# Residual tiles held in the turned rows' order, row norms of later batches on ScalarE, and two x buffers instead of three

## What is computed

```python
x = x + attention(layernorm(x))        # Q, K, V, scores / sqrt(256) * gaussian mask over keys, softmax, V, Wo, bo
x = x + ffn(layernorm(x))              # h = gelu(x @ bw1.T + b1), out = h @ bw2.T + b2, hidden width 1024
# bw = mean(|w|, axis=1) * sign(w), for w1 and w2
```

## Time and profile before

| | |
|---|---|
| median of 3 executions | 1831.75 us |
| lowest, highest | 1826.61, 1834.94 us |
| the profiled execution | 1829.88 us |
| its span | 1828.1 us |
| mean granted TensorE clock | 0.935 of full speed |
| busy: TensorE, VectorE, ScalarE, GpSimd | 1534.9, 1128.3, 885.6, 1243.6 us |
| share of the span | 84%, 62%, 48%, 68% |
| DMA | 121.70 MB, 30.2% of 16 engines |

### The profile page before, as it was taken

One profiled execution on the slowest core, in us unless ns is written; L12 is line 12 of the kernel. 1 busy time (PEld: TensorE's weight loads), 2 busy tenths in 40 slices (PEclk: granted clock), 3 DMA queues, 4 the chain that ended last, 5 costly groups with the idle time before them and its releaser, 6 DMA issues. The chain is left out here.

```text
span 1828.1 us, 20907 instructions
## 1 busy us (share of the span) xinstructions
PE 1534.9 (84%) x7645; PEld 1290.1 (71%) x7645; DVE 1128.3 (62%) x1560; ACT 885.6 (48%) x1118; POOL 1243.6 (68%) x1281
## 2 busy tenths in 40 slices
PE   7787878888788887998788887888798888888887
PEld 5677767777667766777677776776677766776777
DVE  6665666656667565765556656566665666755635
ACT  4554544545455354553535545454554545535443
POOL 4958677576776767767587765867757577675634
PEclk8889998999999899999989988999999999989999
DMA  4504324042340424305143141332404234051220
GB/s 144 111 16 72 91 46 107 9 85 78 56 105 8 85 70 70 93 14 91 58 70 93 32 80 51 70 92 41 105 17 81 81 52 110 1 92 46 47 70 23
DMA packets 103330, 121.70 MB, mean 67 GB/s; under 512 B 11310, under 2 KB 94652, under 8 KB 103228
## 3 DMA queue, kind: packets, MB, share of 16 engines
q1 hardware_dynamic: 103200, 120.37, 30.2%
q10 hardware_dynamic: 28, 0.01, 0.0%
HBM read 20.72 MB, written 16.78 MB: 21 GB/s over the span
## 5 line engine op out<-in xcount | busy, mean ns | idle before, releaser
L379 POOL TENSOR_TENSOR probs<-probs 128x512 fp32r<-128x512 f32 x256 | 351.2, 1390 | 162.9 <-ACT probs L504 162.2
L995 PE MATMUL ps<-sgn,probs 128*128 128x256 f32 x1024 | 284.8, 311 | 99.0 <-DVE ys L729 99.0
L685 DVE STREAM_TRANSPOSE probs<-probs 128x1024 f32<-128x1024 f32 x128 | 159.1, 1243 | 268.5 <-DMA probs<-g 268.1
L504 ACT ACTIVATE probs<-probs 128x1024 fp32r<-128x1024 f32 x128 | 135.6, 1060 | 361.4 <-DVE probs L685 361.4
L995 PEld LDWEIGHTS ps<-sgn,probs 128*128 128x128 f32 x1024 | 222.7, 217 | 110.5 <-issue 72.6
L929 PE MATMUL ps<-probs,xnh 128*128 128x512 f32 x1024 | 283.6, 391 | 0.0
L996 PE MATMUL ps<-sgn,probs 128*128 128x256 f32 x1024 | 279.7, 306 | 0.0
L498 ACT ACTIVATE g<-ps,nmax 128x1024 f32<-128x1024 f32 x128 | 142.6, 1115 | 171.6 <-DVE nmax L677 129.2
L996 PEld LDWEIGHTS ps<-sgn,probs 128*128 128x128 f32 x1024 | 222.4, 217 | 0.8
L929 PEld LDWEIGHTS ps<-probs,xnh 128*128 128x128 f32 x1024 | 190.0, 188 | 38.0
L982 PE MATMUL ps<-rows_h,sgn 128*128 128x512 f32 x512 | 208.0, 406 | 8.6 <-DVE xin L702 6.9
(11 more groups left out here) (112 smaller groups left out, 2967.4 us busy)
## 6 DMA issues: line engine op xcount, KB each, us to landing
probs<-g SPq DMA_DIRECT2D x512, 128.0 KB, 3.5
xin<-in_L_attn_x_dram SPq DMA_DIRECT2D x32, 512.0 KB, 4.6
out_dram<-xin SPq DMA_DIRECT2D x31, 512.0 KB, 3.9
regrouped_rows<-xn SPq DMA_DIRECT2D x120, 128.0 KB, 3.4
w1s<-in_L_ffn_w_dram SPq DMA_DIRECT2D x1, 1024.0 KB, 8.2
w2s<-in_L_ffn_w_dram SPq DMA_DIRECT2D x1, 1024.0 KB, 10.6
mask_bc<-mask_dram SPq DMA_DIRECT2D x1, 512.0 KB, 9.2
out_dram<-xin SPq DMA_DIRECT2D x1, 384.0 KB, 2.5
```

The source lines that it names most:

```text
L379: pool.tensor_tensor(ptl(q)[:, half(n)], pt(q)[:, half(n)], pth(q)[:, half(n)].bitcast(F32), ALU.subtract).then_inc(ptl_set, 1)
L685: dve.transpose(pt(q).rearrange("p (j g c) -> p g j c", j=T, c=QUAD), regrouped(q).rearrange("p (g j r) -> p g j r", j=T, r=QUAD)).then_in ...
L995: pe.matmul(bank, probs[:, 0, r, tile(j)], sgn2[:, j, :], start=j == 0, stop=False)
```

## The change

Six things are changed.

1. **The turned order is kept** for rows, queries and outputs: `hi_rows`, `lo_rows`, `hi_outputs` and `lo_outputs` copy without strides. `hi_keys` and `split_keys` still put the keys in natural order. The residual tiles `xin` are loaded in the order in which outputs now come (`x_res`: partition 8e + u holds the eight rows from 128u + 8e), and stored from it (`out_v`). For the first layernorm a second copy of x in the old order is loaded into one new buffer `xrow`. `xin` has two slots instead of three.
2. **SP's list**: `load_rows(b + 2)` (old order, into `xrow`) and `load(b + 1)` (into `xin`) stand where `load(b + 2)` stood; `regroup_rows(b + 2, n)` moves behind `regroup_probs(b + 1, 1)` and `(b + 1, 2)`.
3. **GpSimd** loses `normalize_attention`; ScalarE does it, four tiles behind each of the first two exponentials of b + 1, with a bias that VectorE makes (`center_attention`). `add_bias` keeps its place and now waits for `x_loaded`. `split_keys(b + 1, 0)` moves behind two `rstd_ffn`, `split_keys(b + 1, 1)` behind `lo_probs(b, 7)`, which moves behind four `rstd_ffn`.
4. **Row sums** of the exponentials are brought into the new order by one small matmul with a permutation matrix `perm` in each `project`; `invert_sums` reads its result.
5. **Query copies** move ahead: ScalarE copies query groups 0 and 1 around `hi_probs(b, 6)`, before `hi_outputs(b, 0)`, and VectorE takes their low parts before `lo_outputs(b, 0)`; `hi_keys` comes after `hi_probs(b, 7)`.
6. **Hidden pairs**: `hidden_pair(b, 3)` moves ahead of `turn_rows_ffn(b, 1)`; the exponentials use the `g` slots shifted by two, and wait for 6, 7 and 8 split pairs instead of 8 each. The preparation of weights before batch 0 is put in another order, the turning of sgn2 moves into batch 0, and mean |w1| is taken later.

```diff
-X_SLOTS = 3
+X_SLOTS = 2
+UNITS = 8
     x_v = x.rearrange("b (p t) d -> b p t d", t=T)
-    out_v = out.rearrange("b (p t) d -> b p t d", t=T)
+    x_res = x.rearrange("b (u e t) d -> b e u t d", u=UNITS, t=T)
+    out_v = out.rearrange("b (u e t) d -> b e u t d", u=UNITS, t=T)
...
-            return g[:, q % G_SLOTS, :]
+            return g[:, (q + 2) % G_SLOTS, :]
...
+            def load_rows(b, n):
+                if b > 0:
+                    sp.wait_ge(xn1_set, T * b)
+                sp.dma_start(xrow[:, n * TH:(n + 1) * TH, :],
+                             x_v[b, :, n * TH:(n + 1) * TH, :]).then_inc(row_loaded[n], 16)
...
                 if b == X_SLOTS - 1:
                     sp.wait_ge(sgn2_set, J // 2)
-                else:
+                elif b >= X_SLOTS:
                     sp.wait_ge(y_stored[n], 16 * (b - X_SLOTS + 1))
                 sp.dma_start(xin[s][:, n * TH:(n + 1) * TH, :],
-                             x_v[b, :, n * TH:(n + 1) * TH, :]).then_inc(x_loaded[s][n], 16)
+                             x_res[b, :, :, n * TH:(n + 1) * TH, :]).then_inc(x_loaded[s][n], 16)
...
                 if b + 2 < B:
                     for n in range(N2):
-                        load(b + 2, n)
+                        load_rows(b + 2, n)
+                if b + 1 < B:
                     for n in range(N2):
-                        regroup_rows(b + 2, n)
-                if b + 1 < B:
+                        load(b + 1, n)
                     for q in range(TH):
                         regroup_probs(b + 1, q)
+                        if q > 0 and q <= N2 and b + 2 < B:
+                            regroup_rows(b + 2, q - 1)
...
             def add_bias(b, tiles):
                 s = b % X_SLOTS
-                pool.wait_ge(xn1_set, T * (b + 1))
                 for t in tiles:
+                    if t % TH == 0:
+                        pool.wait_ge(x_loaded[s][t // TH], 16 * (b // X_SLOTS + 1))
...
                 lo_probs(b, 5)
                 lo_probs(b, 6)
-                if more:
-                    split_keys(b + 1)
                 rstd_ffn(b, 0)
-                lo_probs(b, 7, (0,))
                 rstd_ffn(b, 1)
-                lo_probs(b, 7, (1,))
+                if more:
+                    split_keys(b + 1, 0)
                 rstd_ffn(b, 2)
                 rstd_ffn(b, 3)
+                lo_probs(b, 7)
+                if more:
+                    split_keys(b + 1, 1)
...
                 if more:
                     lo_values(b + 1)
-                if b + 2 < B:
-                    normalize_attention(b + 2)
                 add_b2(b)
...
                 elif b > 0:
-                    act.wait_ge(gl_set, J * b)
+                    act.wait_ge(gl_set, J * b - 2 + q)
...
-                    if q == 0 and b < B - 1:
-                        act.wait_ge(kl_set, N2 * (b + 2))
+                    if q % TH == 0 and b < B - 1:
+                        act.wait_ge(kl_set, N2 * (b + 1) + q // TH + 1)
...
+            def normalize_attention(b, tiles):
+                for t in tiles:
+                    if t == 0:
+                        act.wait_ge(nmr1_set, b)
+                        act.wait_ge(xnl_set, QG * b)
+                    if b >= 2 and t % TH == 0:
+                        act.wait_ge(rows_back[t // TH], 16 * QUADS * (b - 1))
+                    act.activation(xn1_tile(t), in_blocks(xrow[:, t, :]), ACT.Identity, bias=nmr1[:, t:t + 1],
+                                   scale=rstd1[:, t:t + 1]).then_inc(xn1_set, 1)
...
-                dve.tensor_tensor(from_quads(y_row(1, n)), in_quads(flat(ps[:, PV_BANK:PV_BANK + C, :])),
-                                  from_quads(y_row(0, n)).bitcast(F32), ALU.subtract).then_inc(yl_set, 1)
+                dve.tensor_tensor(y_part(1, n), ps[:, PV_BANK:PV_BANK + C, :], y_part(0, n).bitcast(F32),
+                                  ALU.subtract).then_inc(yl_set, 1)
...
                     last.then_inc(o_summed, 1)
+                    if i == 0:
+                        if b == 0 and n == 0:
+                            pe.wait_ge(perm_set, 1)
+                        pe.wait_ge(exp_set, T * b + TH * (n + 1))
+                        pe.matmul(ps[:, PV_BANK, 0:TH], perm[:], rsum[:, n * TH:(n + 1) * TH], start=True,
+                                  stop=True).then_inc(sums_turned, 1)
...
                 hidden_pair(b, 2)
+                hidden_pair(b, 3)
                 turn_rows_ffn(b, 1)
-                hidden_pair(b, 3)
```

More of the change, by code:

```diff
@@ L97, in preln_attention_ffn @@
         ones = sb("ones", [P, P])
-        xin = [sb(f"xin{s}", [P, T, D]) for s in range(X_SLOTS - 1)]
+        perm = sb("perm", [P, P])
+        xrow = sb("xrow", [P, T, D])
+        xin = [sb("xin0", [P, T, D])]
         with ExitStack() as place:
             sw2 = sb("sw2", [P, C, H], F32, place)
-        xin.append(sb(f"xin{X_SLOTS - 1}", [P, T, D]))
+        xin.append(sb("xin1", [P, T, D]))
         g = sb("g", [P, G_SLOTS, S])
@@ L298, in store @@
                 sp.wait_ge(y_set, T * b + done)
-                sp.dma_start(out_v[b, :, tiles, :], xin[b % X_SLOTS][:, tiles, :]).then_inc(y_stored[n], 16)
+                sp.dma_start(out_v[b, :, :, tiles, :], xin[b % X_SLOTS][:, tiles, :]).then_inc(y_stored[n], 16)
             def load(b, n):
@@ L411, in _ @@
             rstd_attention(0)
-            split_keys(0)
+            for n in range(N2):
+                split_keys(0, n)
             lo_values(0)
             rstd_attention(1)
-            normalize_attention(1)
             lo_probs(0, 0)
@@ L552, in _ @@
                 hi_rows(0, n)
+            act.wait_ge(ccol_set, 1)
+            hi_queries(0, range(0, 2))
+            hi_keys(0, 0)
+            hi_queries(0, range(2, QG))
+            hi_keys(0, 1)
+            act.wait_ge(wo_turned, 1)
+            act.activation(woT[:].rearrange("p c d -> p (c d)"), ps[:, 6, :], ACT.Copy).then_inc(woT_set, 1)
+            hi_values(0, range(QG))
             act.wait_ge(w2_loaded, 16)
@@ L578, in _, with signs2 @@
             hi_probs(0, 2)
-            for k in range(J // 2):
-                act.wait_ge(signs_turned, 2 * C + k + 1)
-                act.activation(sgn2[:, 2 * k:2 * k + 2, :], two(ps[:, 4 + k, :]), ACT.Copy).then_inc(sgn2_set, 1)
+            act.wait_ge(signs_set, 1)
+            for j in range(J):
+                act.activation(w1s[:, j, :], w1s[:, j, :], ACT.Abs, scale=1.0 / D,
+                               accum_out=alpha1[:, j:j + 1]).then_inc(alphas_set, 1)
+            def signs2(pairs):
+                for k in pairs:
+                    act.wait_ge(signs_turned, 2 * C + k + 1)
+                    act.activation(sgn2[:, 2 * k:2 * k + 2, :], two(ps[:, QO_BANK + k % 2, :]), ACT.Copy).then_inc(sgn2_set, 1)
             act.wait_ge(alphas_set, C + J)
@@ L767, in _ @@
                 mask_keys(0, n)
+            lo_queries(0, range(QG))
             dve.wait_ge(consts_set, 5)
@@ L819, in batch @@
                 turn_probs(b, 6)
+                if more:
+                    lo_queries(b + 1, range(0, 2))
                 lo_outputs(b, 0)
                 if more:
-                    lo_queries(b + 1, range(0, 2))
+                    lo_queries(b + 1, range(2, 3))
                 turn_probs(b, 7)
                 if more:
-                    lo_queries(b + 1, range(2, QG))
+                    lo_queries(b + 1, range(3, QG))
                 invert_sums(b, 0)
@@ L877, in queries @@
                         pe.wait_ge(ffn_scaled, T * (b - 1))
+                    if k == 0 and b == 1:
+                        pe.wait_ge(sgn2_set, J // 2)
                     if b == 0 and k == 1:
@@ L1073, in batch @@
                     weigh_rows(b, 0, range(6 * i, 6 * i + 6))
+                    if b == 0 and i in (1, 2):
+                        turn_signs2(range(2 * i - 2, 2 * i))
                 if more:
```

188 lines of the change are left out of this document (95 added, 93 removed).

## The result

The changed kernel takes **1991.67 us** (median of 4 executions, 1987.19 to 1993.13), where the kernel before takes 1831.18 in the same comparison: **1.0873 times** as long, 95% interval 1.0843 to 1.0904. It is slower, as forecast, but by 160 us where 34 were forecast, and outside the range of 1808 to 1918.

The account below looks back on a forecast made before the run. TensorE, with the most work, was taken to be bound by waits that return every batch. Per batch 35.0 + 23.6 + 2.2 + 31.7 + 23.0 = 115.5 against 112.6 us; in all +36 on 1829.9: 1866 us, range 1808 to 1918.

Parts of the forecast that it names:

- residual lands: Residual load for the next batch, awaited by GpSimd's add_bias: lands 35.0 us after score tile 4 starts, bounds 33.0 and 36.8.
- landing to transposes: From the load through GpSimd's bias, low parts and keys and ScalarE's norms to the second layernorm's transposes: 23.6 us.
- transposes to first exponential: From the second layernorm's transposes to the next batch's first exponential: 31.7 us instead of 38.1, slow clock 2.2 extra.
- first exponential to next batch: Last stage of a batch, with rows out of SP's way: 23.0 us instead of 29.2, ends 21.4 and 26.
- I take 2.0, as the stretches with loads leave gaps: Delay of the residual load by the two row loads ahead of it: 2.0 us, between nothing and 3.8.
- To it I add what that batch lacks: Last stage: batch 14's 21.4 us plus ScalarE's norms, 4.8 in all, of which about 1.6 delays the third exponential.
- The slow clock: After TensorE's long idle its clock is low: 2.2 us added in front of project(b, 1), bounds 1.2 and 3.4.
- The 3.09: Wait for the last splits before the first exponential, 3.09 us: goes, as the new order needs only six splits.
- 35.0 - 1.75 - 1.6: Transposes to first exponential: 35.0 us less 1.75 for cheaper output copies and 1.6 for the earlier hidden pair 3.
- the fast one: Rival: later stages give back more than the wait costs, -2.9 us a batch, 1785 us; chance 0.20.
- The third: Rival: row loads all go first, landing at +36.8, and splits collide with GpSimd's add_b2; +6.2 a batch, 1912 us; chance 0.18.
- The fourth: Rival: load early enough, GpSimd isn't held up; some -12 us a batch, 1650 to 1700 us; chance 0.02.

Follow-up runs that it names:

- e2: The changed kernel with SP's two residual loads moved ahead of its two row loads: 1942.71 us.
- e3: The changed kernel with residual tiles loaded and outputs stored in plain row order, which computes something else: 1966.63 us.
- e5: e1 with ScalarE's first-layernorm norms cut to 8 of 256 elements a tile from batch 2 on: 1690.75 us.
- e9: e4 with ScalarE's second group of four norms moved from before hi_probs(b + 1, 0) to behind the third exponential: 1624.53 us.
- e4: e1 with both row regroupings moved behind all four regroupings of the probabilities in SP's list: 1624.89 us.
- e6: e1 with GpSimd's add_b2 cut to 8 of 256 elements a tile: 1645.21 us.
- e1: The changed kernel with add_bias taking the tiles of the batch it stands in, in the same two places: 1691.49 us.

## Why the prediction was wrong in size

Its direction held, and so did the mechanism of the wait: the load is late, GpSimd stands still, TensorE idles 20.5 us (19 forecast), and the clock falls. The time was 126 us too low. By its own steps, per batch:

| step | forecast | measured |
|---|---|---|
| residual lands | +35.0 (33.0 to 36.8) | +38.0 |
| landing to transposes | 23.6 | 21.85 |
| transposes to first exponential | 31.7 + 2.2 | 33.45 + 1.65 |
| first exponential to next batch | 23.0 (21.4 to 26) | 27.9 |
| sum | 115.5 | 122.85 |

- **The landing, +3.0.** The step that failed is "I take 2.0, as the stretches with loads leave gaps". The stretches of the earlier trace rows measured two loads of the plain order, with nothing queued behind them. Here the row loads cost 4.3 (e2), and the new address order 2.3 (e3), overlapping. There are no gaps to use: from the first store's issue on, the stores and loads, with the end of the regroupings, take 12.8 us of all 16 engines. The issue of the load is only 0.5 late (+29.0 for +28.45); the rest is its time to landing. A bound that is built from the plain order's busy time left out that the new order keeps the engines longer.
- **First exponential to the next batch, +4.9: the largest error.** "To it I add what that batch lacks", and as that only ScalarE's norms, +1.6. Made shorter by 0.2 us each (e5) or moved, four of eight (e9), they changed no time that can be measured. What batch 14 also lacks is the row regroupings, for which the prediction had one sentence: that they "fall between exponentials". They fall between regroupings that TensorE's rows depend on, and cost 5.5 (e4). The changed kernel's own batch 14 takes 21.9 here, as forecast. The 2.9 of this stage that e6 gives back isn't to be added to the 5.5: the two were not taken out together.
- **Transposes to first exponential, +1.2.** The slow clock was sized well, 1.65 for 2.2. The rest was 33.45 for 31.7. The 3.09 did go: the first exponential follows the table load without a wait. What failed is "35.0 - 1.75 - 1.6": the two gains, 3.35 in all, came to 1.9 (the new table is in 33.3 us behind the transposes in e1, 35.2 before). Which of the two was too large isn't shown. And the 3.09 helps less than it seems: the last two splits still stand in front of the second maximum on VectorE, and the wait is found again one exponential later. From the transposes to the second exponential it is 39.1 us before, 39.7 in e1 and 36.8 in e6. ScalarE's timeline in batch 7:

```profile
1016.39 1.10 ACT L500 ACTIVATE g<-ps,nmax 128x1024 f32<-128x1024 f32 x1
...
1022.66 1.12 ACT L500 ACTIVATE g<-ps,nmax 128x1024 f32<-128x1024 f32 x1 [3.11 <-DVE nmax L710]
```

  From the first to the second it is 1.1 us before and 6.25 after; 2.5 of these are the splits' collision with `add_b2` (3.7 in e6), which the forecast had only as a rival, at +1.5, and ahead of the first exponential.
- **Landing to transposes, -1.75.** Right in its parts: bias 2.79 (3.0), keys 2.82 (3.0), ScalarE 3.9 (4.6).
- **The copies** came out as forecast: `hi_outputs` 1027 ns, `lo_outputs` 1224, and the query wait fell from 65.6 to 10.7. Worth nothing while the wait stands, as forecast. In e1, where it doesn't, the transposes start 4.25 earlier than before (about 5 forecast).
- **Outside batches 1 to 13.** These were to add 38 and add 143: 95.6 of the difference are the 7.35 above, and 9.4 come from setting out from batch 7's period of 112.6 where the mean of the thirteen is 111.84. Batch 0 adds 10.4, forecast 1: SP comes to its loads only at +30, behind the regrouping of tile 7, so that the missing stores gain nothing (landing +38.2). Batch 14 adds 5.8 (5). Batch 15 and the preparation give 2.1, forecast 8.

The marks set for being right: bias rows waiting 420 us (497.8), the wait for `lo_queries` under 15 (10.7) and a clock under 0.935 (0.885) were met; `scale_outputs` under 50 was not (74.6), and the span from the transposes to the next batch, 63.0, passed the 62 that was to show the forecast wrong. It did so because of the last stage, which is where e4 found the time. Of the rivals, the fast one (1785) needed the low end of every term. The third had the late landing and the collision, the latter one exponential too early (e6 brings the first only 0.4 us nearer to the transposes), and stayed too low as it had the same last stage; its own +6.2 a batch gives some 1909, not 1912. The fourth, GpSimd not held up, is what e1 made: 9.4 a batch less and 1691 us, inside its 1650 to 1700, though its "some -12" doesn't follow from the 5 and twice 6 that stand beside it.

A version that beats both kernels is e4_rows_last: the changed kernel with `add_bias(b)` in its own batch and both row regroupings behind the four of the probabilities, 1624.89 us, 11.3% under before.

## What to carry to other kernels

When a buffer is taken away, look for the instruction that will wait for the later load, and at everything queued behind it on that in-order engine: here eight bias additions, needed a whole batch later, held back the keys and cost 300 us that moving two calls gave back. A batch without the removed part is a good measure of a stage only if it is asked what else that batch lacks, DMA issues on SP among it. A wait that disappears because its condition was relaxed should be looked for at the next instruction in the chain.
